# Routing of the second mixture shared out over four engines, and TensorE's joints filled with further rows and products

## The chip, the cores and the metric

The kernel runs on one core of one Trainium2 chip. The metric is the device time of one execution in microseconds (us). The core's engines are TensorE (PE; its weight loads are shown apart, as PEld), VectorE (DVE), ScalarE (ACT), GpSimd (POOL) and SyncE (SP), which issues DMAs. Each works through its own list of instructions in order and waits for others only through semaphores.

## The reference

An audio tower on 32 sequences of 166 positions (5312 tokens) of width 128, in float32:

```
h = tok(x)                          # three frames of 64, one dense layer
h = h + lru(norm(h))                # complex linear recurrence, 256 states
h = h + mixture0(norm(h))           # 16 experts, top 2
h = h + sparse_attention(norm(h))   # 8 heads, 25 chosen queries
h = h + mixture1(norm(h))           # 64 experts, top 42
```

`mixture0` picks two experts per token by `gate_logits`. For each expert it takes the mean of `silu(x w1)` over the expert's tokens, multiplies that mean by `w2`, and each token adds its two experts' results with its two routing weights. So its last step is a product of a 16 x 128 table `y_mean` and 16 weights per token.

`mixture1` is, for each token:

```
logits = x @ router_w + router_b                  # 64
probs = softmax(logits)
top_w, top_idx = top_k(probs, 42);  top_w = softmax(top_w)
comb = zeros(64).at[top_idx].set(top_w)
h = gelu(x @ w1[e] + b1[e]);  y = h @ w2[e] + b2[e]
out = sum over e of y[e] * comb[e]
```

## The kernel before, in words

Tokens lie along the free dimension: `k.h` and `k.hc` are 128 x 5376 (42 tiles of TW = 128 tokens; 14 chunks of CW = 384). `k.hc` holds the tokens less their mean, `k.rstd` one factor per token. The stages follow each other with all engines meeting between them. The order inside a stage is written out by hand: one function per engine, each a fixed list.

**The end of `first_mixture`.** ACT has put the tokens' 16 routing weights into rows 0 to 15 of `k.hc`, called `rt`. PE sums the table into bank 7 (L1105), DVE copies it to `ym`, 16 x 128 (L1048). Then PE multiplies `ym` by 384 tokens of `rt` for each of the 14 chunks (L1112), each into one of four banks, and DVE adds the bank to `k.h` (L1051). PE may be four chunks ahead. A float32 product appears as two instructions in the trace. After it comes `norm_statistics` "n3" (L411 to L449), in which POOL also splits experts' weights that SP fetches by DMA from the start of that stage (L1869 to L1877), and then the attention.

**The routing in `second_mixture`.** NP = 7 passes of two chunks (six tiles, PT) each. For a chunk c: POOL lays `rstd` on a diagonal (L778), PE spreads it over the partitions (L784), DVE multiplies it with `k.hc` to `ut` (`apply`, L792), ACT and POOL split `ut` into two float16 halves (`u_highs` L2109, `u_lows` L2073), and PE makes the 3 x 64 logits (`logits_of`, L2274). For a pass p, on DVE, in this order:

1. two copies of the logits out of the banks with the sign changed and the router's bias subtracted, into `row` (L2195), and the minimum of it (L2200);
2. `apply` of chunk 2p+2; the eight largest and their replacement (L2202, L2203); two small steps between ACT's two exponentials (L2205, L2206); `apply` of chunk 2p+3;
3. two more rounds of the eight largest and their replacement (L2209 to L2212), after which the 22 dropped experts carry a mark in `work`;
4. the masking of the exponentials by that mark (L2214), their sum (L2215) and its reciprocal (L2216). POOL multiplies them to `shares` (L2088).

ACT in pass p: first exponentials (L2125), `u_highs(2p+2)`, the copy of the turned shares of pass p-1 (L2113), the copy of the bias products of pass p-2 (L2117), second exponentials (L2135), `u_highs(2p+3)`.

PE's list in pass p: `logits_of(2p)`, spread of chunk 2p+2, `logits_of(2p+1)`, spread of chunk 2p+3, `turn(p-1)` (the transposes of the shares of pass p-1, L2283), `biases(p-2)` (the turned shares times `b2`, L2291). After pass 6 there follow `turn(6)`, `biases(5)` and `biases(6)`. `biases` of a pass waits until ACT has copied out those of the pass before.

**The expert loop** follows: 64 experts in four groups, six blocks of 896 tokens. PE multiplies up (`up_of`, L2322) and down (`down_of`, L2339), ACT, POOL and DVE do the gelu, the split into float16 halves and the sum. `WARM` is 8; `warm_up` is called at the start of some stages and multiplies constants into bank 7, which nobody reads.

Of the kernel before, what the change touches and what calls it, by code (L numbers as in the profile page):

```python
# [7 lines left out]
ALU = mybir.AluOpType  # L8
# [38 lines left out]
CUT = -2.5e38  # L47
# [24 lines left out]
def warm_up(nc, k):  # L72


    for _ in range(WARM):
        nc.tensor.matmul(k.bank[:, 7, :], k.sel[:, 0, :], k.sel[:, 0:4, :].rearrange("p a b -> p (a b)"), start=True, stop=True)
# [719 lines left out]
def first_mixture(nc, k):  # L796
# [6 lines left out]
    with ExitStack() as ctx:  # L803
# [40 lines left out]
        ym = sb("ym", [E0, 128])  # L844
        xt = sb("xt", [128, RING, 2, ST], F16)
        rt = k.hc[0:E0, :]

        gate_in = sem("gate_in")
        made = sem("made")
# [57 lines left out]
        @block.gpsimd  # L907
        def _(pool):
            g = nc.gpsimd
            g.memset(before[:], 1.0).then_inc(made, 1)  # L910
            g.memset(every[:], 1.0).then_inc(made, 1)
            g.memset(going[:], 1.0).then_inc(made, 1)
            g.memset(hsum[:], 0.0).then_inc(made, 1)
            g.iota(line[:], [[1, NST]], base=0, channel_multiplier=0, allow_small_or_imprecise_dtypes=True).then_inc(made, 1)
            g.iota(tile_no[:], [[0, 1]], base=0, channel_multiplier=1, allow_small_or_imprecise_dtypes=True).then_inc(made, 1)
            pool.wait_ge(made, 6)
            g.memset(going[:, :, 0:1], 0.0).then_inc(made, 1)
            g.affine_select(out=before[:], in_=before[:], compare_op=ALU.is_ge, fill=0.0, base=-1,
                            pattern=[[1, 128]], channel_multiplier=-1).then_inc(made, 1)
# [34 lines left out]
        def _(dve):  # L954
# [91 lines left out]
            v.tensor_copy(hsum[:, :, 0:E0 * E0:E0 + 1], k.bank[:, 1, 0:FC * E0].rearrange("p (f e) -> p f e", f=FC)).then_inc(gathered, 1)  # L1046
            dve.wait_ge(y_ready, 1)
            v.tensor_copy(ym[:], k.bank[0:E0, 7, 0:128]).then_inc(y_kept, 1)  # L1048
# [5 lines left out]
        def _(pe):  # L1054
# [54 lines left out]
            for c in range(NCW):  # L1109
                if c >= 4:  # L1110
                    pe.wait_ge(added, c - 3)
                t.matmul(k.bank[:, c % 4, 0:CW], ym[:], rt[:, span(c)], start=True, stop=True).then_inc(out, 1)  # L1112
# [835 lines left out]
def second_mixture(nc, k, out):  # L1948
# [9 lines left out]
    with ExitStack() as ctx:  # L1958
# [17 lines left out]
        rb = sb("rb", [128, E1])  # L1976
# [6 lines left out]
        ex = sb("ex", [128, 2, PT, E1])  # L1983
        shares = sb("shares", [128, NTW, E1])
# [18 lines left out]
        exp2 = sem("second_exp")  # L2003
        shared = sem("share_ready")
# [35 lines left out]
        @block.sync  # L2040
        def _(sp):
            for dst, src in ((router[:], a["router"]), (rb[:], a["router_b"].partition_broadcast(128)), (b1[:], a["e_b1"]),
                             (b2[:], a["e_b2"])):
                sp.dma_start(dst, src).then_inc(small_in, 16)

            def weights(grp):
                if grp >= 2:
                    sp.wait_ge(y_ready[1], (grp - 1) * NWB * GE + KEEP)
                for m in range(4):
                    sp.dma_start(k.weights[:, grp % 2, m], k.kept[grp - 1, :, m]).then_inc(group_in, 16)  # L2050

            def store(tb):

                cols = slice(tb * WB, min((tb + 1) * WB, T))
                sp.wait_ge(h_added, tb + 1)
                sp.dma_start(out[:, cols], k.h[:, cols]).then_inc(stored, 16)

            for grp in range(1, NG):
                weights(grp)
            for tb in range(NWB):  # L2060
                store(tb)
            sp.wait_ge(stored, 16 * NWB)

        @block.gpsimd
        def _(pool):
# [15 lines left out]

            ahead(0)
            ahead(1)
            for p in range(NP):
                ahead(2 * p + 2)
                ahead(2 * p + 3)
                pool.wait_ge(shared, p + 1)
                g.tensor_tensor(shares[:, p * PT:(p + 1) * PT], ex[:, p % 2], red[:, p % 2, 5].unsqueeze(2).broadcast_to([128, PT, E1]),  # L2088
                                ALU.mult).then_inc(share_ready, 1)
# [11 lines left out]
        def _(act):  # L2101
# [16 lines left out]

            u_highs(0)
            u_highs(1)  # L2120
            for p in range(NP):
# [15 lines left out]
                u_highs(2 * p + 3)  # L2137
            comb_copies(NP - 1)
# [23 lines left out]
        def _(dve):  # L2162
# [27 lines left out]
            for p in range(NP):  # L2190
                j = p % 2
                r = red[:, j]
                for q in range(2):
                    dve.wait_ge(logits, 2 * p + q + 1)
                    last = v.scalar_tensor_tensor(row[:, j, q * PT // 2:(q + 1) * PT // 2, 0:E1],  # L2195
                                                  k.bank[:, 4 + q, 0:PT // 2 * E1].rearrange("p (n e) -> p n e", e=E1), -1.0,
                                                  rb[:].unsqueeze(1).broadcast_to([128, PT // 2, E1]), ALU.mult, ALU.subtract)
                    last.then_inc(copied, 1)
# [3 lines left out]
                tiles(lambda m: v.max(best[:, m], row[:, j, m]))  # L2202
                tiles(lambda m: v.match_replace(work[:, m], best[:, m], row[:, j, m], MARK))  # L2203
# [3 lines left out]
                apply(2 * p + 3)  # L2207
                for last_round in (False, True):
                    tiles(lambda m: v.max(best[:, m], work[:, m]))  # L2209
                    if last_round:  # L2210
                        link(v.memset(best[:, :, drop % 8:8], SENT))
                    tiles(lambda m: v.match_replace(work[:, m], best[:, m], work[:, m], MARK))  # L2212
                dve.wait_ge(exp2, p + 1)
# [3 lines left out]
            dve.sem_inc(second_of[0], 2)  # L2217
            for q in range(2):
                dve.sem_inc(y_added[q], 1)
            dve.wait_ge(acc_ready, NP)  # L2220
# [9 lines left out]
            def add(it):  # L2230
# [3 lines left out]
                tb, e = it // GE % NWB, it // (GE * NWB) * GE + it % GE  # L2234
                for q, (start, end) in enumerate(PARTS_Y):
# [30 lines left out]
        def _(pe):  # L2266
            t = nc.tensor

            def logits_of(c):
# [3 lines left out]
                for q in range(CW // TW):  # L2273
                    last = t.matmul(k.bank[:, 4 + c % 2, q * E1:(q + 1) * E1], ut[:, c % 2, q * TW:(q + 1) * TW], router[:],  # L2274
                                    start=True, stop=True)
# [31 lines left out]
            turn(NP - 1)  # L2307
            biases(NP - 2)
            biases(NP - 1)
# [64 lines left out]

            pe.wait_ge(k.expert_weights.split, GROUP)
            pe.wait_ge(acc_ready, NP)
            pe.sem_inc(y_ready[1], KEEP)
            up_of(0, 0, 0, 0)
# [111 lines left out]
```

## Time and profile before

| | us |
|---|---|
| median of 3 runs | 2136.46 (2134.52 to 2138.97) |
| the profiled execution | 2138.86 |
| its span in the trace | 2137.1 |
| PE busy | 1885.2 (88%) |
| DVE busy | 1676.4 (78%) |
| ACT busy | 1388.1 (65%) |
| POOL busy | 1349.4 (63%) |

The span runs from the first to the last instruction of the trace; the time of the execution contains a little more around it. PEclk is the clock that was granted to TensorE as a share of full speed: 1.00 is 2.4 GHz and 0.50 is 1.2 GHz; a number between them is a mean over a stretch. In the timeline a row may stand for several like instructions (x6 and so on), the time is then from the first's start to the last's end, and brackets show how long the engine sat idle before it and who released it. "Issue" is idle time for which the trace shows no other engine.

### The profile page before, as it was taken

How to read it: one execution, taken by the hardware profiler on the slowest of the kernel's cores; microseconds unless marked ns; L12 is line 12 of the kernel's file. 1: busy time of each engine (PE TensorE's matmuls, PEld its weight loads, DVE VectorE, ACT ScalarE, POOL GpSimd, SP SyncE). 2: the span in 40 equal slices, each digit the busy share in tenths (PEclk: the TensorE clock that was granted, in tenths of full speed). 3: DMA queues.
4: the chain of work that ended last, by engine and by line, in shares of the span. 5: the costliest groups of instructions: out<-in, count | busy, mean ns of one | idle time of the engine just before them, and what ended most of it. 6: DMA issues, size and time to landing. Idle time of an engine off the chain costs nothing.

```text
span 2137.1 us, 50727 instructions
## 1 busy us (share of the span) xinstructions
PE 1885.2 (88%) x17146; PEld 1354.1 (63%) x17146; DVE 1676.4 (78%) x4764; ACT 1388.1 (65%) x2070; POOL 1349.4 (63%) x1026
## 2 busy tenths in 40 slices
PE   7889300888998987799999999999999999999998
PEld 5556200455657875567777777777777777777776
DVE  4775730853567767879999999999999999999998
ACT  3112350742443544488888888888888888888886
POOL 2100177005970003288989999988898989888887
PEclk9999655997998996599999999999999999999999
DMA  3612181612320002000000100000200000000000
GB/s 90 179 40 99 56 302 59 121 39 65 98 79 1 1 1 82 1 1 2 0 0 0 76 6 1 0 0 1 81 2 0 0 0 2 2 10 10 10 10 18
DMA packets 73497, 82.63 MB, mean 39 GB/s; under 512 B 38564, under 2 KB 56516, under 8 KB 71684
## 3 DMA queue, kind: packets, MB, share of 16 engines
q1 hardware_dynamic: 70660, 75.19, 11.6%
q0 software_dynamic: 2688, 5.44, 0.8%
q8 instruction: 94, 1.54, 0.3%
q14 instruction: 55, 0.45, 0.1%
HBM read 42.97 MB, written 29.20 MB: 34 GB/s over the span
## 4 chain that ended last, share of the span: by engine, by line
PE 56%; DVE 3%; issue 1%; POOL 0%; ACT 0%; ACTq 0%; DVEq 0%; POOLq 0%
PE bank L2339 29%; PE bank L2322 27%; DVE m_work L2212 1%; DVE m_best L2209 0%; DVE m_work L2203 0%; DVE m_ut L792 0%; PE bank L2291 0%; DVE m_best L2202 0%; DVE m_ex L2214 0%; ACT m_h L2153 0%; DVE h L2250 0%; POOL m_h L2098 0%; DVE m_red L2215 0%; DVE m_row L2195 0%; PE bank L784 0%
## 5 line engine op out<-in xcount | busy, mean ns | idle before, releaser
L2339 PEld LDWEIGHTS bank<-weights,m_h 128*128 128x128 f16 x10752 | 639.1, 98 | 190.0 <-DVE hc L2241 91.6
L2098 POOL TENSOR_TENSOR m_h<-m_hidden,m_h 128x896 f16<-128x896 f32 x384 | 725.2, 1888 | 31.9
L2241 DVE SCALAR_TENSOR_TENSOR hc<-bank,m_shares,hc 128x128 f32<-128x128 f32 x2688 | 727.0, 342 | 4.1 <-PE bank L2339 4.1
L2339 PE MATMUL bank<-weights,m_h 128*128 128x128 f16 x10752 | 724.4, 219 | 2.4 <-POOL m_h L2098 2.4
L2150 ACT ACTIVATE m_hidden<-bank,m_b 128x896 f32<-128x896 f32 x384 | 386.7, 1007 | 184.2 <-PE bank L2322 184.1
L2228 DVE TENSOR_TENSOR m_h<-bank,m_h 128x896 f16<-128x896 f32 x384 | 419.2, 1092 | 108.8 <-ACT m_h L2153 108.8
L2096 POOL TENSOR_SCALAR m_h<-m_hidden 128x896 f16<-128x896 f32 x384 | 359.8, 937 | 111.5 <-ACT m_hidden L2150 83.0
L2322 PE MATMUL bank<-m_u_first,weights 128*128 128x448 f16 (+1 forms) x1536 | 417.8, 354 | 6.9 <-DVE h L2250 5.5
L2322 PE MATMUL bank<-m_u_second,weights 128*128 128x448 f16 (+1 forms) x1536 | 417.4, 353 | 0.0
L2147 ACT ACTIVATE bank<-bank,m_b 128x896 f32<-128x896 f32 x384 | 377.2, 982 | 0.4 <-PE bank L2322 0.4
L2153 ACT ACTIVATE m_h<-bank 128x896 f16<-128x896 f32 x384 | 348.7, 908 | 0.0
L2322 PEld LDWEIGHTS bank<-m_u_second,weights 128*128 128x128 f16 x1536 | 150.5, 98 | 141.3 <-issue 1.8
L926 POOL DMA_INDIRECT expert_slots<-m_u_tok,m_slot x84 | 87.4, 1041 | 68.5 <-DVE m_slot L1018 43.2
L2322 PEld LDWEIGHTS bank<-m_u_first,weights 128*128 128x128 f16 x1536 | 118.1, 98 | 10.0 <-DVE h L2250 6.4
L1089 PE MATMUL bank<-m_xt,weights 128*128 128x384 f16 x344 | 65.6, 336 | 64.4 <-issue 64.4
L1042 DVE TENSOR_REDUCE m_part<-bank 128x2 f32<-128x768 f32 x86 | 74.7, 941 | 58.9 <-ACT bank L951 58.9
L2067 POOL MEMSET m_row<- 128x96 f32 x1 | 0.2, 178 | 185.7 <-POOLq L371 185.7
L951 ACT ACTIVATE bank<-bank 128x768 f32<-128x768 f32 x86 | 64.4, 794 | 64.4 <-PE bank L1089 64.4
L1089 PEld LDWEIGHTS bank<-m_xt,weights 128*128 x344 | 34.0, 99 | 96.2 <-issue 83.2
L1869 POOL CAST weights<-ew_raw 128x1024 f16<-128x1024 f32 x8 | 8.3, 1037 | 131.6 <-DMA ew_raw<-e_w_dram 131.6
L433 DVE TENSOR_TENSOR hc<-h,bank 128x332 f32 (+2 forms) x60 | 31.5, 525 | 52.8 <-PE bank L411 52.6
L543 POOL TENSOR_TENSOR lru_diag<-ident,rstd 128x332 f32<-128x332 f32 x16 | 12.8, 817 | 87.5 <-PE bank L684 61.6
(328 smaller groups left out, 2143.7 us busy)
## 6 DMA issues: line engine op xcount, KB each, us to landing
weights<-expert_factors SPq DMA_DIRECT2D x12, 1024.0 KB, 8.6
expert_slots<-lru_zeros SPq DMA_DIRECT2D x1, 8256.0 KB, 31.9
lw_raw<-e_w_dram SPq DMA_DIRECT2D x16, 512.0 KB, 4.8
expert_factors<-lw_made SPq DMA_DIRECT2D x16, 512.0 KB, 4.6
ew_raw<-e_w_dram SPq DMA_DIRECT2D x16, 512.0 KB, 4.4
lru_wst<-w_dram SPq DMA_DIRECT2D x16, 256.0 KB, 2.7
weights<-w_dram SPq DMA_DIRECT2D x1, 4096.0 KB, 12.7
expert_factors<-ew_made SPq DMA_DIRECT2D x8, 512.0 KB, 3.1
```

The source lines that it names most:

```text
L926: g.indirect_dma_start(out=k.slots, out_offset=bass.IndirectOffsetOnAxis(ap=slot[0:rows_n, m, n:n + 1], axis=0), in_=u_tok[0:rows_n, n].re ...
L1042: v.tensor_reduce(part[:, j // PARTS, j % PARTS * FP:(j % PARTS + 1) * FP], set_banks(j), X, ALU.add).then_inc(summed, 1)
L1089: last = t.matmul(set_banks(n)[:, f % FP], w0_parts[m][:, bass.ds(expert * FF0 + f * 128, 128)], xt[:, j % RING, m], start=(m == 0), stop= ...
L2096: g.tensor_scalar(h1[:, x, 0], hidden[:, x], 1.0 - SHARE, 1.0, ALU.mult, ALU.mult).then_inc(first_of[1], 1)
L2098: g.tensor_tensor(h1[:, x, 1], hidden[:, x], h1[:, x, 0], ALU.subtract).then_inc(second_of[1], 1)
L2147: sc.activation(banks0(x), banks0(x), ACT.Gelu, bias=b1[:, bass.ds(grp * GE + e, 1), 0]).then_inc(gelu[0], 1)
L2150: sc.activation(two(hidden[:, x % 2]), banks1, ACT.Gelu, bias=b1[:, bass.ds(grp * GE + e, 1), 1]).then_inc(gelu[1], 1)
L2153: sc.activation(two(h0[:, x, 0]), banks0(x), ACT.Copy, scale=1.0 - SHARE).then_inc(first_of[0], 1)
L2228: v.tensor_tensor(two(h0[:, x, 1]), banks0(it), two(h0[:, x, 0]), ALU.subtract).then_inc(second_of[0], 1)
L2241: last = v.scalar_tensor_tensor(acc[:, m * TW:(m + 1) * TW], y[q][:, (n - start) * TW:(n - start + 1) * TW], shares[:, m, e:e + 1], acc[:, ...
L2322: last = t.matmul(bank[:, q], k.weights[:, grp % 2, m, at], uu[:, bass.ds(tb * WB + q * HW, HW)], start=(m == 0), stop=(m == 1))
L2339: last = t.matmul(y[q][:, (n - start) * TW:(n - start + 1) * TW], factors[:, m, n * TW:(n + 1) * TW], k.weights[:, grp % 2, 2 + m, at], st ...
```

## The change

- `first_mixture`: `ym` becomes a 128 x 128 tile that POOL clears; the table is in its first 16 rows; the 14 products take all 128 rows of `k.hc` instead of `rt`.
- Routing: ACT copies the logits with the sign changed (`rows`), and PE adds the bias by a further product of one row per tile. For passes 0 to 5 POOL marks the kept experts and masks the exponentials; the sum and reciprocal of pass p-1 are done by DVE within pass p, behind its second `apply`, and POOL makes the shares of pass p-1 then. Pass 6 keeps the old order.
- The joint to the expert loop: PE's list is now `biases(5)`, 24 products of constants into bank 0, the first expert product, `turn(6)`, `biases(6)`. Semaphore increments and DVE's wait for the bias copies move.

Cut to its core:

```diff
-def warm_up(nc, k):
-    for _ in range(WARM):
-        nc.tensor.matmul(k.bank[:, 7, :], ...)
+def warm_up(nc, k, bank=7, count=WARM):
+    for _ in range(count):
+        nc.tensor.matmul(k.bank[:, bank, :], ...)
# first_mixture
-        ym = sb("ym", [E0, 128])
+        ym = sb("ym", [128, 128])
+            g.memset(ym[:], 0.0).then_inc(cleared, 1)
+            dve.wait_ge(cleared, 1)
-            v.tensor_copy(ym[:], k.bank[0:E0, 7, 0:128]).then_inc(y_kept, 1)
+            v.tensor_copy(ym[0:E0], k.bank[0:E0, 7, 0:128]).then_inc(y_kept, 1)
-                t.matmul(k.bank[:, c % 4, 0:CW], ym[:], rt[:, span(c)], start=True, stop=True).then_inc(out, 1)
+                t.matmul(k.bank[:, c % 4, 0:CW], ym[:], k.hc[:, span(c)], start=True, stop=True).then_inc(out, 1)
# second_mixture, SP: (rb[:], a["router_b"].partition_broadcast(128)) becomes (rb[:], a["router_b"]), rb [1, E1]
# POOL
+            def shares_of(p):
+                pool.wait_ge(shared, p + 1)
+                g.tensor_tensor(shares[...], ex[:, p % 2], red[:, p % 2, 5]..., ALU.mult).then_inc(share_ready, 1)
             for p in range(NP):
                 ahead(2 * p + 2)
+                if p:
+                    shares_of(p - 1)
                 ahead(2 * p + 3)
-                pool.wait_ge(shared, p + 1)
-                g.tensor_tensor(shares[...], ...).then_inc(share_ready, 1)
+                if p < NP - 1:
+                    pool.wait_ge(chosen, p + 1)
+                    pool.wait_ge(exp2, p + 1)
+                    g.tensor_scalar(kept[:], work[:, :, 0:E1], CUT, 1.0, ALU.is_gt, ALU.mult).then_inc(marked, 1)
+                    pool.wait_ge(marked, p + 1)
+                    g.tensor_tensor(ex[:, p % 2], kept[:], ex[:, p % 2], ALU.mult).then_inc(masked, 1)
+            shares_of(NP - 1)
# ACT
+            def rows(p):
+                for q in range(2):
+                    act.wait_ge(logits, 2 * p + q + 1)
+                    sc.activation(row[...], k.bank[:, 4 + q, ...], ACT.Copy, scale=-1.0).then_inc(copied, 1)
+            rows(0)
             for p in range(NP):
                 ...
                 u_highs(2 * p + 3)
+                rows(p + 1)
# DVE
             for p in range(NP):
-                for q in range(2):
-                    dve.wait_ge(logits, 2 * p + q + 1)
-                    last = v.scalar_tensor_tensor(row[...], k.bank[:, 4 + q, ...], -1.0, rb[:]..., ALU.mult, ALU.subtract)
-                    last.then_inc(copied, 1)
                 dve.wait_ge(copied, 2 * p + 2)
                 ...
+                if p:
+                    dve.wait_ge(marked, p)
                 tiles(lambda m: v.match_replace(work[:, m], best[:, m], row[:, j, m], MARK))
                 ...
                 apply(2 * p + 3)
+                if p:
+                    dve.wait_ge(masked, p)
+                    link(v.tensor_reduce(red[:, 1 - j, 4], ex[:, 1 - j], X, ALU.add))
+                    v.reciprocal(red[:, 1 - j, 5], red[:, 1 - j, 4]).then_inc(shared, 1)
                 for last_round in (False, True):
                     ...
+                if p < NP - 1:
+                    dve.sem_inc(chosen, 1)
+                    continue
                 dve.wait_ge(exp2, p + 1)
                 ...
-            dve.sem_inc(second_of[0], 2)
-            dve.wait_ge(acc_ready, NP)          # now in add(), before its first sum
# PE
-                    last = t.matmul(k.bank[...], ut[...], router[:], start=True, stop=True)
+                    t.matmul(tile, ut[...], router[:], start=True, stop=False)
+                    last = t.matmul(tile, k.ones[0:1, :], rb[:], start=False, stop=True)
-            turn(NP - 1)
-            biases(NP - 2)
-            biases(NP - 1)
+            biases(NP - 2)
             pe.wait_ge(k.expert_weights.split, GROUP)
+            pe.wait_ge(u_low, NCW)
+            pe.sem_inc(second_of[0], 2)
+            pe.sem_inc(y_ready[1], KEEP)
+            warm_up(nc, k, 0, 3 * WARM)
+            up_of(0, 0, 0, 0)
+            turn(NP - 1)
+            biases(NP - 1)
             pe.wait_ge(acc_ready, NP)
-            pe.sem_inc(y_ready[1], KEEP)
-            up_of(0, 0, 0, 0)
```

## Rows read from the trace of the kernel before

**Rows 1.** the page, parts 2 (tenths of full clock in 40 slices) and 4 (the chain)

```profile
PEclk9999655997998996599999999999999999999999
...
PE bank L2339 29%; PE bank L2322 27%; DVE m_work L2212 1%; DVE m_best L2209 0%; DVE m_work L2203 0%; DVE m_ut L792 0%; PE bank L2291 0%; DVE m_best L2202 0%; DVE m_ex L2214 0%; ACT m_h L2153 0%; DVE h L2250 0%; POOL m_h L2098 0%; DVE m_red L2215 0%; DVE m_row L2195 0%; PE bank L784 0%
```

**Rows 2.** windows, first joint (length, busy of PE, PEld, DVE, ACT, POOL, PEclk)

```profile
476.00:478.00 2.00, 1.83 (x6) 1.14 (x7) 0.91 (x3) 0.00 (x0) 0.00 (x0) 1.00 0.00 0
480.00:493.00 13.00, 12.37 (x20) 5.90 (x18) 5.70 (x11) 0.00 (x0) 0.00 (x0) 0.50 0.00 0
```

**Rows 3.** windows of one routing pass and of the first expert products

```profile
867.18:878.73 11.55, 10.02 (x35) 7.33 (x34) 11.14 (x66) 6.41 (x22) 4.22 (x5) 0.50 0.00 1
909.70:915.10 5.40, 5.37 (x15) 2.14 (x16) 0.17 (x1) 4.50 (x6) 0.79 (x1) 0.50 0.00 0
```

**Rows 4.** timeline of the same routing pass (start, us, engine, line, instruction)

```profile
867.18 0.58 DVE L2195 SCALAR_TENSOR_TENSOR m_row<-bank,m_rb 128x192 f32<-128x192 f32 x2
...
867.80 0.55 DVE L2200 TENSOR_REDUCE m_red<-m_row 128x6 f32<-128x384 f32 x1
...
868.23 1.49 PE L2283 MATMUL bank<-ident,m_shares 128*64 128x128 f32 x6 [0.49 <-POOL m_shares L2088]
...
868.38 0.35 ACT L2125 ACTIVATE m_ex<-m_row,m_red 128x64 f32<-128x64 f32 x1 [4.12 <-DVE m_red L2200]
...
870.39 0.51 ACT L2109 ACTIVATE m_u_first<-m_ut 128x384 f16<-128x384 f32 x1
...
871.82 0.54 DVE L792 TENSOR_TENSOR m_ut<-hc,bank 128x384 f32<-128x384 f32 x1
...
872.50 1.54 PE L2274 MATMUL bank<-m_router,m_ut 128*128 128x64 f32 x6
...
873.84 1.59 PE L784 MATMUL bank<-m_diag,ones 128*128 128x384 f32 x2
...
875.22 1.38 PE L2274 MATMUL bank<-m_router,m_ut 128*128 128x64 f32 x6
...
876.98 1.02 DVE L2214 SCALAR_TENSOR_TENSOR m_ex<-m_work,m_ex 128x384 f32<-128x384 f32 x1
...
878.04 0.55 DVE L2215 TENSOR_REDUCE m_red<-m_ex 128x6 f32<-128x384 f32 x1
...
878.89 0.83 POOL L2088 TENSOR_TENSOR m_shares<-m_ex,m_red 128x384 f32<-128x384 f32 x1 [1.31 <-DVE m_red L2216]
```

**Rows 5.** timeline, minima of passes 1 and 6, and the last joint

```profile
833.61 0.55 DVE L2200 TENSOR_REDUCE m_red<-m_row 128x6 f32<-128x384 f32 x1
...
890.43 0.55 DVE L2200 TENSOR_REDUCE m_red<-m_row 128x6 f32<-128x384 f32 x1
...
893.52 0.90 DVE L2209 MAX8 m_best<-m_work 128x8 f32<-128x72 f32 x6
...
905.88 2.90 PE L2291 MATMUL bank<-m_b,m_comb 64*128 64x128 f32 x12 [0.99 <-ACT hc L2117]
...
909.73 0.90 PE L2322 MATMUL bank<-m_u_first,weights 128*128 128x448 f16 x2 [0.95 <-issue]
...
911.17 0.95 PE L2322 MATMUL bank<-m_u_first,weights 128*128 128x448 f16 x2
```

**Rows 6.** timeline around the first joint

```profile
477.12 1.84 DVE L1051 TENSOR_TENSOR h<-h,bank 128x384 f32<-128x384 f32 x3 [1.00 <-PE bank L1112]
...
492.40 0.56 DVE L1051 TENSOR_TENSOR h<-h,bank 128x384 f32<-128x384 f32 x1 [0.72 <-PE bank L1112]
...
515.30 2.12 POOL L1877 TENSOR_TENSOR weights<-ew_left,weights 128x1024 f16<-128x1024 f32 x1
...
518.01 0.22 DVE L449 TENSOR_TENSOR rstd<-n_st 83x64 f32<-83x64 f32 x1
```

**Rows 7.** weight loads of L1112 and L2274 (duration ns min/median/max)

```profile
L1112 PEld LDWEIGHTS bank<-hc,m_ym x28: 181/328/328, 476.2 to 490.9; 16*128 16x128 f32 x28
...
L2274 PEld LDWEIGHTS bank<-m_router,m_ut x84: 186/333/338, 818.7 to 886.4; 128*128 128x128 f32 x84
```

More of the change, by code:

```diff
@@ L69, in load_table @@
     nc.scalar.activation(k.cells[:, n + 1:n + 2], k.cells[:, 0:1], function)
-def warm_up(nc, k):
-    for _ in range(WARM):
-        nc.tensor.matmul(k.bank[:, 7, :], k.sel[:, 0, :], k.sel[:, 0:4, :].rearrange("p a b -> p (a b)"), start=True, stop=True)
+def warm_up(nc, k, bank=7, count=WARM):
+    for _ in range(count):
+        nc.tensor.matmul(k.bank[:, bank, :], k.sel[:, 0, :], k.sel[:, 0:4, :].rearrange("p a b -> p (a b)"), start=True, stop=True)
 STEP = 4
@@ L848, in first_mixture @@
         gate_in = sem("gate_in")
+        cleared = sem("outputs_cleared")
         made = sem("made")
@@ L1975, in second_mixture @@
         router = sb("router", [128, E1])
-        rb = sb("rb", [128, E1])
+        rb = sb("rb", [1, E1])
         b1 = sb("b1", [128, E1, HC])
@@ L1983, in second_mixture @@
         ex = sb("ex", [128, 2, PT, E1])
+        kept = sb("kept", [128, PT, E1])
         shares = sb("shares", [128, NTW, E1])
@@ L2003, in second_mixture @@
         exp2 = sem("second_exp")
+        marked = sem("kept_marked")
+        masked = sem("dropped_masked")
+        chosen = sem("dropped_marked")
         shared = sem("share_ready")
@@ L2041, in _ @@
         def _(sp):
-            for dst, src in ((router[:], a["router"]), (rb[:], a["router_b"].partition_broadcast(128)), (b1[:], a["e_b1"]),
+            for dst, src in ((router[:], a["router"]), (rb[:], a["router_b"]), (b1[:], a["e_b1"]),
                              (b2[:], a["e_b2"])):
@@ L2080, in ahead @@
                     norm.pool_diagonal(pool, c + 2, c % 2)
+            def shares_of(p):
+                pool.wait_ge(shared, p + 1)
+                g.tensor_tensor(shares[:, p * PT:(p + 1) * PT], ex[:, p % 2], red[:, p % 2, 5].unsqueeze(2).broadcast_to([128, PT, E1]),
+                                ALU.mult).then_inc(share_ready, 1)
             ahead(0)
@@ L2085, in _ @@
                 ahead(2 * p + 2)
+                if p:
+                    shares_of(p - 1)
                 ahead(2 * p + 3)
-                pool.wait_ge(shared, p + 1)
-                g.tensor_tensor(shares[:, p * PT:(p + 1) * PT], ex[:, p % 2], red[:, p % 2, 5].unsqueeze(2).broadcast_to([128, PT, E1]),
-                                ALU.mult).then_inc(share_ready, 1)
+                if p < NP - 1:
[5 more added lines that the diff above has]
+            shares_of(NP - 1)
             with pool.Fori(0, NG * NWB * GE // 2) as i:
@@ L2117, in biases @@
                 sc.activation(two(acc[:, 2 * p * CW:2 * (p + 1) * CW]), k.bank[:, 6:8, 0:CW], ACT.Copy).then_inc(acc_ready, 1)
+            def rows(p):
+                if p >= NP:
+                    return
+                for q in range(2):
+                    act.wait_ge(logits, 2 * p + q + 1)
+                    sc.activation(row[:, p % 2, q * PT // 2:(q + 1) * PT // 2, 0:E1],
+                                  k.bank[:, 4 + q, 0:PT // 2 * E1].rearrange("p (n e) -> p n e", e=E1), ACT.Copy,
+                                  scale=-1.0).then_inc(copied, 1)
             u_highs(0)
             u_highs(1)
+            rows(0)
             for p in range(NP):
@@ L2192, in _ @@
                 r = red[:, j]
-                for q in range(2):
-                    dve.wait_ge(logits, 2 * p + q + 1)
-                    last = v.scalar_tensor_tensor(row[:, j, q * PT // 2:(q + 1) * PT // 2, 0:E1],
-                                                  k.bank[:, 4 + q, 0:PT // 2 * E1].rearrange("p (n e) -> p n e", e=E1), -1.0,
-                                                  rb[:].unsqueeze(1).broadcast_to([128, PT // 2, E1]), ALU.mult, ALU.subtract)
-                    last.then_inc(copied, 1)
                 dve.wait_ge(copied, 2 * p + 2)
@@ L2234, in add @@
                 tb, e = it // GE % NWB, it // (GE * NWB) * GE + it % GE
+                if it == 0:
+                    dve.wait_ge(acc_ready, NP)
                 for q, (start, end) in enumerate(PARTS_Y):
@@ L2273, in logits_of @@
                 for q in range(CW // TW):
-                    last = t.matmul(k.bank[:, 4 + c % 2, q * E1:(q + 1) * E1], ut[:, c % 2, q * TW:(q + 1) * TW], router[:],
-                                    start=True, stop=True)
+                    tile = k.bank[:, 4 + c % 2, q * E1:(q + 1) * E1]
+                    t.matmul(tile, ut[:, c % 2, q * TW:(q + 1) * TW], router[:], start=True, stop=False)
+                    last = t.matmul(tile, k.ones[0:1, :], rb[:], start=False, stop=True)
                 last.then_inc(logits, 1)
```

## The prediction

> **What bounds the kernel now.** The page comes first: the chain that ended last lies for 29% and 27% of the span on the two TensorE lines of the expert loop, every other line has 1% or less [rows 1]. That loop runs from about 921 us to the end at the full clock (the trailing 9s of the PEclk row) with PE busy without a gap, and the change touches no instruction of it. What can move is in the places where the PEclk row shows 5s. I read two of them in windows and then in the timeline.
>
> The first is the joint at the end of the first mixture. PE enters it at granted clock 1.00, and while it multiplies operands of only 16 rows it is busy in 12.37 of 13.00 us at 0.50 [rows 2]: the clock fell under an engine that hardly ever waited. There VectorE waits for PE once per chunk.
>
> The second is the routing before the expert loop, seven passes p. In a window of one pass in the middle VectorE is busy 11.14 of 11.55 us; PE is busy 10.02 of them, at 0.50 [rows 3]. The timeline of the same pass gives the prices [rows 4]. So VectorE is the bound, but PE at its slow rate has only 1.5 us of slack, and this decides the forecast. After the last pass PE, ACT and POOL hand on to each other until the first expert product at 909.73 [rows 5].
>
> **The change, part by part.**
>
> *First joint.* The 14 products get 128 rows instead of 16 (the further rows meet zero weights). Three adds at the full rate take 1.84 us, so (1.84 - 0.56) / 2 = 0.64 us per chunk; the last add now ends at 492.40 + 0.56 = 492.96 [rows 6]. If PE stays at full clock, the last ends at 477.12 + 13 x 0.64 + 0.56 = 486.00: 7.0 us earlier. The next stage, the third normalisation, then also starts at full clock, but POOL's weight pieces in it hang on a DMA issued after the joint: they end at 517.42 and VectorE's last step at 518.23 [rows 6], so POOL is late next and only 0.8 us more can be kept. Together -7.8. Bounds: 0 (zero weights count for nothing and the clock falls as before) and -7.8. I take -7.8: up to 478 the clock is still 1.00, carried by products of 128 rows, and only the rows differ. The clearing of the larger tile on POOL is awaited some 250 us later: nothing.
>
> *Routing, VectorE's own work.* Each pass loses two bias-adding copies (867.18 to 867.80: 0.62) and, in the first six, the masking (876.98 to 878.04: 1.06, where the work of a single 384-element instruction, 0.55 as in the reduce behind it, fills half) [rows 4]. So 9.87 instead of 11.55 if VectorE stayed the bound. POOL takes over with a marking and a masking of 384 elements, 0.4 (bound 0.83) + 0.83; it is idle then and has them ready long before VectorE asks.
>
> *Routing, the cycle that closes.* Before, the share of pass p-1 was ready at the end of pass p-1, so PE could turn it and multiply the biases while VectorE began pass p. Now its sum comes in the middle of pass p, after the second `apply`. PE's order is unchanged: the turn of p-1 and the biases of p-2 stand ahead of the logits of chunks 2p+2 and 2p+3, and pass p+1 cannot start without those. So one pass becomes a loop through all engines, each term from [rows 4]:
> - the last logit to VectorE through ACT's copy of 192 elements: 0.46 with hand-offs (an exponential of 64 takes 0.35, a copy of 384 takes 0.51; nearer the middle);
> - VectorE from the minimum (867.80) to the end of the second `apply` (871.82 + 0.54 = 872.36): 4.56;
> - sum and reciprocal until POOL starts, 878.04 to 878.89: 0.85; POOL's share 0.83 and its hand-off to PE 0.06: 0.89;
> - turn and biases, 868.23 to 872.50: 4.27;
> - logits: six instructions take 1.34 (872.50 to 873.84). Each product gets a partner of one row, so twelve: 2.68;
> - spread of rstd, 873.84 to 875.22: 1.38; the second logits 2.72.
>
> Sum 17.81 us instead of 11.55. The price of the one-row products is not shown. From below it is 0; from above the 0.24 of a bias product (12 in 2.90 [rows 5]). A weight load of 16 rows takes 328 ns and one of 128 rows 333 [rows 7]: rows don't make it cheaper, so I take the 0.223 of a router product.
>
> From p=1 to p=2 there are no biases yet (14.95), three passes are full, from p=5 to p=6 no spread is left (16.43): 14.95 + 3 x 17.81 + 16.43 = 84.8, against 890.43 - 833.61 = 56.8 now [rows 5]. That is +28.0, and +14.6 with free one-row products. The first pass has no earlier share to wait for; its later logits (about +1.1) and its lighter work cancel: 0.
>
> *Last joint.* Now: from the last minimum 890.43 to PE's first expert product 909.73, 19.3 us [rows 5]. After: VectorE reaches the rounds 3.09 later (893.52), sum and share 1.74, so PE's turn starts at 4.83; turn and biases 9.1; ACT copies them out before PE may go on, 1.0 (the idle time in the row of 905.88); the biases of p=5 until 13.0. Then 24 warm-up products of 512 columns. Four expert products of 448 columns start within 911.17 - 909.73 = 1.44 us at 0.50 [rows 5], 0.36 each, so one of 512 takes 0.41; that dense stretch stayed at 0.50 for 5.4 us [rows 3]. So 13 warm-up products are slow and 11 take half: 7.7, until 20.7. The first expert products 0.8, the turn 0.7 (until 22.2), ACT's two copies with hand-offs 1.8, the last biases 1.4 at full clock (2.9 at half), ACT's copy 0.9: 26.3 instead of 19.3, so +7.0. The warm-up stands ahead of the last turn in PE's queue, and the share it needs is ready about 6 us before PE gets there. A warm start gives back about 1.0 of the 5.4 us ramp (bounds 0 and 2.7, if all of it were PE's own).
>
> The moved waits and semaphore increments and the smaller bias load (the pass starts on a later DMA anyway) cost nothing.
>
> Sum: -7.8 + 28.0 + 7.0 - 1.0 = +26.2. The profiled execution took 2138.86 us (span 2137.1 and 1.8 around it), 2.4 above the median of the runs; 2136.46 + 26.2 = 2163.
>
> **A rule of the skill against this.** In [rows 4] PE works without a break from the turn at 868.23 to the end of the second logits near 876.6, and the window has 0.50 throughout [rows 3]. The Trainium skill, page "TensorE: Matmul & The Clock Gate", section "Why this matters for your kernels", says that steady work releases the clock and that only long gaps between bursts bring it down. By that rule PE's unbroken run in the new pass, 11 us, would go at full rate; the trace doesn't bear it out, with longer busy shares than the new loop has.
>
> **The rivals.**
> - *PE at full clock in the routing.* For it: the stretch is longer and unbroken. Against it: PE's share falls to 12.4 of 17.8 us (70%, now 87% at 0.50), and half of the added products have one row, while 16 rows lost the clock in [rows 2]. PE's terms halve (11.05 to 5.5): 12.3 per full pass, 59.4 for the five, so +2.6; last joint 19.9, +0.6; -1.0; -7.8: -5.6, 2131. If the clock is full for only part of each pass, half-way: 2147.
> - *VectorE stays the bound* (the late share finds PE free). It needs the turn not to stand ahead of logits that the next pass waits for; the order in the code says it does. About 1.5 less per pass, -7.5; +7.0; -1.0; -7.8: -9.3, 2127.
> - *The rows don't hold the clock*: the joint's 7.8 stay away, 2171. For it: most of the weights are zero.
> - *One-row products cost nothing*: 2163 - 13.4 = 2150.
>
> The sign turns where the loop is shorter than about 12.5 us.
>
> **How the numbers follow.** The low-clock loop has 0.83, with the joint failing in 0.12 of it and cheap one-row products in 0.05; partly full clock 0.07; full clock 0.05; VectorE the bound 0.05. Range 2148 to 2171: from cheap products (or a partly full clock) to the failing joint. A measurement tells about 0.2% (4.3 us) from no change. Faster: the last two cases, with little from the third, 0.09; within 0.2%: 0.03; slower: 0.88.
>
> **What would show it.** In the changed profile: L1112 with a chunk every 0.64 us and granted clock 1.00; in the routing PEclk 0.5 and a minimum of row every 17 to 18 us, VectorE waiting for ACT's copies there and ACT for PE's logits; PE's turn of the last share starting 6.3 us behind the minimum instead of beside it; a warm-up of 24 at the end with the last turn behind it. It is wrong if the passes are 12.5 us or less apart, or if PEclk in the routing is near 1.

## The result, and the profile after

| | before | after |
|---|---|---|
| median of 4 runs each, us | 2135.94 (2134.52 to 2138.97) | 2176.72 (2173.63 to 2193.05) |
| the profiled execution | 2138.86 | 2173.63 |
| its span | 2137.1 | 2171.9 |
| PE / DVE / ACT / POOL busy | 1885.2 / 1676.4 / 1388.1 / 1349.4 | 1911.7 / 1667.7 / 1394.0 / 1365.2 |

The ratio is 1.0178, with a 95% interval from 1.0138 to 1.0218: slower, as forecast, but by 40.8 us where 26.2 were forecast, and outside the range. The two profiled executions lie 34.8 apart. Without a head start that the change did not make it would be 40.2: the copy of the table `ym` starts at 470.47 after and at 475.84 before, 5.4 earlier, though ahead of it only POOL's clearing of the tile was added (in the profiles of the other kernels it starts anywhere between 470.7 and 493.0).

The page of the changed kernel, parts 2 and 4, answers to [rows 1]:

```profile
PEclk9999655998989985589999999999999999999999
...
PE bank L2372 28%; PE bank L2355 26%; PE bank L2311 1%; PE bank L2310 1%; PE bank L2327 1%; PE bank L784 1%; PE bank L2319 0%; DVE m_work L2230 0%; PE bank L76 0%; DVE m_best L2227 0%; POOL m_shares L2093 0%; DVE m_ut L792 0%; ACT m_h L2184 0%; DVE h L2285 0%; POOL m_h L2118 0%
```

Before, the first lines behind the expert loop were VectorE's; now they are PE's one-row product (L2311), router product (L2310), bias product (L2327) and spread (L784). Part 1 says the same: VectorE lost 8.7 us of work and PE gained 26.5.

The windows of the changed kernel (columns as in [rows 2] and [rows 3]): the first joint, the first routing pass up to its minimum, one pass in the middle, and the start of the expert loop in steps of 5 us:

```profile
471.70:480.70 9.00, 8.40 (x27) 4.61 (x25) 7.76 (x14) 0.00 (x0) 0.00 (x0) 1.00 0.00 0
804.60:813.70 9.10, 9.10 (x28) 7.00 (x27) 0.56 (x1) 1.29 (x4) 3.35 (x4) 0.50 1.00 419
860.24:879.88 19.64, 14.60 (x47) 10.69 (x47) 9.49 (x63) 7.18 (x24) 6.71 (x7) 0.50 0.00 0
935.00:940.00 5.00, 5.00 (x25) 2.48 (x23) 0.00 (x0) 0.00 (x0) 0.00 (x0) 0.90 0.00 0
940.00:945.00 5.00, 2.42 (x15) 1.84 (x14) 0.00 (x0) 2.62 (x4) 0.00 (x0) 0.79 0.00 0
945.00:950.00 5.00, 4.62 (x13) 1.40 (x12) 1.09 (x1) 4.78 (x7) 1.65 (x2) 0.53 0.00 0
```

A pass takes 19.64 us instead of 11.55, with no engine busy for more than 14.60 of them: a loop through all engines, and not one engine's work. The timeline of that loop, PE first, then ACT, VectorE and POOL:

```profile
846.82 1.49 PE L2319 MATMUL bank<-ident,m_shares 128*64 128x128 f32 x6 [5.04 <-POOL m_shares L2093]
848.23 2.93 PE L2327 MATMUL bank<-m_b,m_comb 64*128 64x128 f32 x12
851.09 0.69 PE L2310 MATMUL bank<-m_router,m_ut 128*128 128x64 f32 x2
851.71 0.69 PE L2311 MATMUL bank<-m_rb,ones 1*128 1x64 f32 x2
852.32 0.69 PE L2310 MATMUL bank<-m_router,m_ut 128*128 128x64 f32 x2
...
854.79 1.65 PE L784 MATMUL bank<-m_diag,ones 128*128 128x384 f32 x2
856.23 0.53 PE L2310 MATMUL bank<-m_router,m_ut 128*128 128x64 f32 x2
...
859.77 1.65 PE L784 MATMUL bank<-m_diag,ones 128*128 128x384 f32 x2
...
859.87 0.33 ACT L2144 ACTIVATE m_row<-bank 128x192 f32<-128x192 f32 x1 [4.65 <-PE bank L2311]
...
860.24 0.55 DVE L2225 TENSOR_REDUCE m_red<-m_row 128x6 f32<-128x384 f32 x1 [9.84 <-ACT m_row L2144]
...
864.26 0.54 DVE L792 TENSOR_TENSOR m_ut<-hc,bank 128x384 f32<-128x384 f32 x1
864.73 0.54 DVE L2238 TENSOR_REDUCE m_red<-m_ex 128x6 f32<-128x384 f32 x1
...
865.57 0.83 POOL L2093 TENSOR_TENSOR m_shares<-m_ex,m_red 128x384 f32<-128x384 f32 x1 [0.46 <-DVE m_red L2239]
```

The brackets close the loop: PE waits 5.04 us for POOL's share, ACT 4.65 for PE's last logits, VectorE 9.84 for ACT's copy, and POOL waits for VectorE's sum. Where the 40.2 us lie, by the starts of the same instruction in both traces:

| stretch | before | after | difference | forecast |
|---|---|---|---|---|
| `ym` copy to rstd of the second mixture | 475.84 to 814.44 | 470.47 to 800.40 | -8.7 | -7.8 |
| rstd to the first minimum | 8.09 | 13.33 | +5.2 | 0 |
| passes 0 to 1 | 11.08 | 10.38 | -0.7 | 0 |
| passes 1 to 6 | 56.82 | 93.77 | +37.0 | +28.0 |
| last minimum to the expert loop | 19.30 | 26.85 | +7.6 | +7.0 |
| the expert loop to the end | 1227.4 | 1227.2 | -0.2 | -1.0 |

### The profile page after: what moved, and what is told of

Same layout as the page of the kernel before. It is cut to its first block, busy times and chain, and to the rows that moved or that the text cites. A ratio compares the mean times of both kernels' runs of the same rounds, so it can differ in the third digit from the quotient of the medians.

```text
span 2171.9 us, 50963 instructions
## 1 busy us (share of the span) xinstructions
PE 1911.7 (88%) x17254; PEld 1374.7 (63%) x17254; DVE 1667.7 (77%) x4744; ACT 1394.0 (64%) x2084; POOL 1365.2 (63%) x1039
## 4 chain that ended last, share of the span: by engine, by line
PE 59%; DVE 1%; issue 1%; ACT 1%; POOL 1%; ACTq 0%; DVEq 0%; POOLq 0%
PE bank L2372 28%; PE bank L2355 26%; PE bank L2311 1%; PE bank L2310 1%; PE bank L2327 1%; PE bank L784 1%; PE bank L2319 0%; DVE m_work L2230 0%; PE bank L76 0%; DVE m_best L2227 0%; POOL m_shares L2093 0%; DVE m_ut L792 0%; ACT m_h L2184 0%; DVE h L2285 0%; POOL m_h L2118 0%
```

## The experiments

Baselines: the kernel before took 2137.95 beside full_row_bias, paired_bias, bias_dve and lag, 2137.54 beside joint1, joint1_tail, lag_bias_dve_tail and no_warm, and 2137.07 beside old_share and joint1_64. The diffs are cut to their core. A product means one call in the code, which is two instructions in the trace. Two theories stand at the start. *Change of rows*: a product of one row costs more than its like when it stands between products of 128. *Accumulation*: a second product into the same bank region costs more, whatever its rows. A third, *the clock*, would blame the granted clock, but that is 0.50 in the pass of before and of after alike.

**full_row_bias**: the changed kernel, with the router's bias in row 0 of a zeroed tile of 128 rows.

```diff
-        rb = sb("rb", [1, E1])
+        rb = sb("rb", [128, E1])            # cleared, the bias in row 0
-                    last = t.matmul(tile, k.ones[0:1, :], rb[:], start=False, stop=True)
+                    last = t.matmul(tile, k.ones[:], rb[:], start=False, stop=True)
```

> The changed kernel, but the bias product has 128 rows: ones of 128 rows against a tile with the bias in row 0 and zeros below. In the changed kernel three router products with their one-row partners take 3.68 us where twelve instructions of equal price would take 2.68. Theory 'change of rows' (each change between 128-row and 1-row weights costs some 0.17 us): 2.68 per chunk, minima of the middle passes 17.6 us apart instead of 19.64, the execution some 10 us shorter. Theory 'accumulation' (the second product waits for the first in the same tile): nothing moves, 3.68 and 19.64.

Measured: 2162.99 in one run. The middle passes are 17.55 us apart (17.56, 17.55, 17.55). PE's rows of this kernel, to be held beside those of the changed one above:

```profile
851.36 0.63 PE L2314 MATMUL bank<-m_rb,ones 128*128 128x64 f32 x2
851.78 0.63 PE L2313 MATMUL bank<-m_router,m_ut 128*128 128x64 f32 x2
852.21 0.64 PE L2314 MATMUL bank<-m_rb,ones 128*128 128x64 f32 x2
```

Like product follows like after 0.42 us, where it was 0.62 with one row. With 127 rows of zeros more, the kernel is some 14 us faster. A chunk's six products (three of the router, three of the bias) take 2.61 (850.88 to 853.49) instead of 3.70 (851.09 to 854.79). The accumulation is as before, so that theory is out. The weight loads show the same. First the changed kernel, then this one:

```profile
851.70 0.50 PEld L2311 LDWEIGHTS bank<-m_rb,ones 1*128 1x128 f32 x2
852.32 0.50 PEld L2310 LDWEIGHTS bank<-m_router,m_ut 128*128 128x128 f32 x2
```

```profile
851.25 0.55 PEld L2314 LDWEIGHTS bank<-m_rb,ones 128*128 128x128 f32 x2
851.68 0.55 PEld L2313 LDWEIGHTS bank<-m_router,m_ut 128*128 128x128 f32 x2
```

Where the rows change, the load starts together with its own product (851.70 and 851.71), when the product before is all but over (851.09 + 0.69 = 851.78, an end that the profile models). Where all have 128, it starts 0.11 ahead of its product (851.25 and 851.36) and lies beside the one before. That the late load is what costs the time is not shown; the two go together.

**paired_bias**: one-row products, but the middle tile in the opposite order (router, bias, bias, router, router, bias), which leaves four changes of rows per chunk instead of six.

```diff
+                    first, then = (ut[...], router[:]), (k.ones[0:1, :], rb[:])
+                    if q == 1:
+                        first, then = then, first
+                    t.matmul(tile, *first, start=True, stop=False)
+                    last = t.matmul(tile, *then, start=False, stop=True)
```

> The changed kernel with the order of the two products turned round in the middle tile of each chunk (router, bias, bias, router, router, bias): four changes of rows per chunk instead of six, the same accumulations. 'Change of rows': 0.34 us less per chunk, minima 18.95 apart, some 3.5 us shorter. 'Accumulation': 19.64, no shorter.

Measured: 2174.98 in one run, 1.7 below the changed kernel's median where 3.5 were expected, too little to read from one run; the middle passes are 18.88 apart (18.95 expected). Three kernels give three points: 0, 4 and 6 changes per chunk, 2.61, 3.32 and 3.70 us per chunk. That is 0.18 us for each change, twice: 0.71 / 4 and 1.09 / 6. The theory of the changes of rows holds with its number, for one row among products of 128; no other pair of row counts was tried.

**bias_dve**: the changed kernel with the logits copied and biased by VectorE, as before the change; the late share, POOL's mask and both joints stay.

```diff
-            rows(0)
-                rows(p + 1)
-                    last = t.matmul(tile, k.ones[0:1, :], rb[:], start=False, stop=True)
+                for q in range(2):
+                    dve.wait_ge(logits, 2 * p + q + 1)
+                    last = v.scalar_tensor_tensor(row[...], k.bank[:, 4 + q, ...], -1.0, rb[:]..., ALU.mult, ALU.subtract)
```

> The changed kernel with the bias back on VectorE: its two copies per pass as before, no one-row products, no copies on ACT; masking on POOL and the late share stay. Theory 'the loop through the late share sets the pass': router products 1.34 per chunk, minima 19.64 - 2 x 2.34 + 0.1 = 15.1 us apart, the five passes 23 us shorter and the first some 4 us, so about 2149. Rival 'the one-row products are all of the loss, the late share is harmless': VectorE is the bound again at 10.5 to 10.9 per pass, about 2128.

Measured: 2150.9 in two runs, ratio 1.0074 (1.0045 to 1.0103); passes of 15.61, 15.02, 15.02. The late share closes the loop alone; the change of sign does not need the one-row products.

**old_share**, the complement: the kernel before with only ACT's copies and the one-row products.

```diff
+            def rows(p):                     # ACT, as in the changed kernel
-                for q in range(2):           # the two copies on DVE
-                    last = t.matmul(k.bank[...], ut[...], router[:], start=True, stop=True)
+                    t.matmul(tile, ut[...], router[:], start=True, stop=False)
+                    last = t.matmul(tile, k.ones[0:1, :], rb[:], start=False, stop=True)
```

> The kernel before with one part of the change alone: ACT copies the logits, PE adds the bias by one-row products; the share stays at the end of its pass, masking on VectorE, both joints as before. The one-row products' measured price adds 2.36 us per chunk to TensorE (3.70 for the logits of a chunk instead of 1.34), so its 10.02 us per pass become 14.7. By 'TensorE's own work is then the bound' the minima stand 14.7 to 15.2 us apart in the middle passes, and the time is about 2155. By 'the bias products lie in slack that only the late share takes away' the minima stay near 11.6 and the time near 2140. By the forecast's price (1.34 per chunk) they would stand about 12.7 apart, 2144.

Measured: 2147.36, ratio 1.0047 (1.0025 to 1.0068); passes 1 to 6 are 11.31, 11.81, 14.39, 14.40 and 13.11 apart. The profiled execution was a long one (2159.74; its routing starts some 11 us later than before's), so only the passes are read from it. Its windows and a few rows:

```profile
850.00:865.00 15.00, 15.00 (x56) 11.10 (x56) 13.77 (x88) 9.20 (x32) 5.34 (x7) 0.61 0.00 1
865.00:880.00 15.00, 15.00 (x49) 11.16 (x48) 13.31 (x81) 7.58 (x26) 6.19 (x7) 0.50 0.00 1
880.00:900.00 20.00, 20.00 (x64) 14.85 (x64) 12.38 (x72) 8.62 (x32) 5.40 (x7) 0.50 0.01 2
```

```profile
863.08 0.43 PE L2281 MATMUL bank<-m_rb,ones 1*128 1x64 f32 x2
863.44 0.43 PE L2280 MATMUL bank<-m_router,m_ut 128*128 128x64 f32 x2
...
867.08 0.69 PE L2281 MATMUL bank<-m_rb,ones 1*128 1x64 f32 x2
867.70 0.69 PE L2280 MATMUL bank<-m_router,m_ut 128*128 128x64 f32 x2
```

PE is the bound here, busy without a gap, and 14.40 is its own work (10.02 [rows 3] and twice 3.70 - 1.34 give 14.7). The passes before are shorter for two reasons: 11.31 (at 0.50) has no biases yet, and 11.81 has the PE instructions of a full pass, with part of them at the high clock (0.64 over that pass; 0.36 from one product to the next instead of 0.62). So the time came out at 2147 and not near 2155. The four kernels make a square of middle passes: neither part 11.55, one-row products alone 14.40, late share alone 15.02, both 19.64. Alone, the one-row products cost 2.85, since 1.5 us of them go into time that PE had free. With the loop closed they stand on the path, all twelve instructions: 19.64 - 15.02 = 4.62, 0.385 each.

**lag**: the changed kernel, with turns, biases and their copies one pass later in PE's and ACT's lists, so that PE finds each share ready. ACT's first exponentials also wait for the shares of pass p-2, whose place they take.

```diff
-                if p:
-                    turn(p - 1)
-                if p >= 2:
-                    biases(p - 2)
+                if p >= 2:
+                    turn(p - 2)
+                if p >= 3:
+                    biases(p - 3)
```

> The changed kernel with the turns, the biases and ACT's copies of them moved one pass later in the lists (in pass p the turn of p-2 and the biases of p-3), so that no logits stand behind a share that is still being made. PE has the same products. Theory 'loop': the pass falls from 19.64 to PE's own work, 1.41 + 2.86 + 2 x 3.68 + 2 x 1.4 = 14.5 us; 22 us shorter over the passes, perhaps 2 to 4 given back in the tail, so about 2157. Rival 'PE's added work sets the pass by itself': minima stay about 19 apart, 2175.

Measured: 2142.34, ratio 1.0016 (0.9998 to 1.0035); passes 1 to 6 are 10.38, 10.01, 11.35, 14.39 and 13.11 apart. (The profiled execution took 2159.81; its copy of `ym` starts only at 493.0, so again only the routing is read from it.) The steady pass is PE's own work, as expected; the total came out 15 us better. One part is the clock: the pass of 11.35, at 0.65, has the PE instructions of the one of 14.39, at 0.50. Another is that the early passes are lighter in this order: 10.38, at 0.50, has no turn and no biases. Windows of this kernel:

```profile
850.00:860.00 10.00, 9.91 (x32) 7.13 (x31) 9.15 (x61) 5.31 (x22) 6.60 (x7) 0.51 0.01 2
860.00:870.00 10.00, 9.58 (x37) 6.96 (x37) 9.55 (x64) 6.25 (x24) 6.72 (x7) 0.66 0.00 1
870.00:880.00 10.00, 10.00 (x41) 7.32 (x40) 8.24 (x52) 5.61 (x17) 6.72 (x7) 0.67 0.00 1
880.00:890.00 10.00, 10.00 (x36) 7.77 (x34) 8.00 (x57) 5.83 (x19) 5.36 (x6) 0.50 0.01 2
```

All but 4.4 of the 40.8 us are gone by the order of two lists (and the higher clock that part of it was granted), with every instruction of the change still there: the loop, and not the work, was most of the price.

**joint1**: the kernel before with the first joint's 128 rows alone (diff as in the change).

> The kernel before with the first joint alone changed: the cleared 128-row tile and all 128 rows of hc. Theory 'rows hold the clock': the 14 chunks take 0.64 us each at granted clock 1.00 and the execution is 8 us shorter (7.0 in the joint, 1 in the stage behind it), ratio 0.9963. Rival 'the gain is given back in the next stage, where POOL waits for its DMA': under 3 us.

Measured: 2130.66, ratio 0.9961 (0.9937 to 0.9984). This part is a gain of 6.9 us. **joint1_64** takes 64 rows:

```diff
-                t.matmul(k.bank[:, c % 4, 0:CW], ym[:], k.hc[:, span(c)], ...)
+                t.matmul(k.bank[:, c % 4, 0:CW], ym[0:64], k.hc[0:64, span(c)], ...)
```

> The kernel before with the first joint's products of 64 rows (48 of them with zero weights) instead of 16 or 128. If any number of rows above 16 holds the clock, the granted clock stays 1.00 and the 14 chunks take 8.9 us. If half the rows count for half, the clock falls on the way, and the joint takes between 10 and 15.8 us (15.8 is what 16 rows took).

Measured: 2131.84 in one run. The joint in the timeline and two windows of this kernel:

```profile
477.00 8.94 DVE L1054 TENSOR_TENSOR h<-h,bank 128x384 f32<-128x384 f32 x14 [1.00 <-PE bank L1115]
```

```profile
480.00:484.00 4.00, 4.00 (x14) 2.34 (x13) 3.46 (x7) 0.00 (x0) 0.00 (x0) 1.00 0.00 0
484.00:488.00 4.00, 2.65 (x10) 1.41 (x9) 1.99 (x5) 1.49 (x2) 0.00 (x0) 1.00 0.21 26
```

64 rows, 48 of them with zero weights, hold the clock as 128 do; 16 do not [rows 2].

**no_warm**: the changed kernel without the 24 warm-up products (the call of `warm_up(nc, k, 0, 3 * WARM)` deleted).

> The changed kernel without the 24 warm-up products. Theory 'the warm-up stands in front of the last turn': the turn of pass 6 starts when its share is ready, at half clock; from the last minimum to the first expert product behind the copies 21.5 us instead of 26.85, 5.3 us shorter than the changed kernel, about 2170. Rival 'the warm-up pays for itself at full clock': not shorter, 2175 or more.

Measured: 2167.56 in two runs, ratio 1.0129 (1.0081 to 1.0178), 9.2 less than the changed kernel, with an interval about as wide; the traces tell more: from the last minimum (917.61) to the expert loop (937.55) 19.94 us instead of 26.85, and from there to the end 1226.3 instead of 1227.2. The warm-up costs its 6.9 us and gives nothing back.

**joint1_tail**: joint1, with the last joint in the new order but without warm-up, and with ACT's gelu table loaded ahead of the last shares.

```diff
# ACT
-            comb_copies(NP - 1)
             biases(NP - 2)
+            load_table(nc, k, 0, ACT.Gelu)
+            comb_copies(NP - 1)
             biases(NP - 1)
             act.sem_inc(second_of[1], 2)
-            load_table(nc, k, 0, ACT.Gelu)
# PE: biases(5), up_of(0, 0, 0, 0), turn(6), biases(6)
```

> The kernel before with the first joint, and with the last joint in another order and without warm-up products: the biases of pass 5 as soon as PE is free, then the first expert product, then the turn and the biases of pass 6; ACT loads the gelu table before it waits for the last turn. The routing passes are as before. Theory 'the chain behind the last share is what costs, and nothing may stand in front of it': from the last minimum to the first gelu 16.4 us instead of 21.1, so 4.7 shorter than the first joint alone, about 2125. Rival 'the order hardly matters, ACT's copies are late anyway': under 1.5.

Measured: 2123.8, ratio 0.9922 (0.9893 to 0.9951). The last joint of this kernel:

```profile
889.31 2.89 PE L2294 MATMUL bank<-m_b,m_comb 64*128 64x128 f32 x12 [0.99 <-ACT hc L2120]
892.13 0.93 PE L2322 MATMUL bank<-m_u_first,weights 128*128 128x448 f16 x2
...
893.66 1.14 PE L2286 MATMUL bank<-ident,m_shares 128*64 128x128 f32 x6
895.69 1.60 PE L2294 MATMUL bank<-m_b,m_comb 64*128 64x128 f32 x12 [0.89 <-ACT m_comb L2116]
898.19 0.93 PE L2322 MATMUL bank<-m_u_first,weights 128*128 128x448 f16 x2 [0.90 <-ACT hc L2120]
```

```profile
893.07 1.28 ACT L69 ACT_TABLE_LOAD   x1
...
897.33 0.81 ACT L2120 ACTIVATE hc<-bank 128x768 f32<-128x768 f32 x1 [1.69 <-PE bank L2294]
898.03 0.98 ACT L2150 ACTIVATE bank<-bank,m_b 128x896 f32<-128x896 f32 x1
```

From the last minimum (883.54) to the first gelu 14.5 us; 21.1 before (890.43 to 911.52), 28.2 after (917.88 to 946.09). The 1.28 us table load now lies in ACT's idle time, and the biases of the last pass run at a granted clock of 1.00 (1.60 us instead of 2.90). The clock doesn't stay: the expert products behind them start 0.36 us apart again, as at 0.50.

**lag_bias_dve_tail**: joint1_tail's joints, the late share, POOL's mask, the lag, and the bias on VectorE (the diffs of bias_dve, lag and joint1_tail together).

> All that the runs point to: the first joint, masking on POOL with the late share, turns and biases one pass later in the lists, the bias on VectorE, no one-row products, no warm-up, and the gelu table loaded before the last turn. Theory 'loop': VectorE is the bound again, at 11.55 - 1.06 = 10.5 us per pass, PE's 10.0 beside it; the five passes take about 53 us instead of 56.8. The tail has turn 5 and biases 4 and 5 in front of turn 6 and gains nothing on before. About 2125. Rival: PE at 10 of 10.5 us becomes the bound through its waits and the passes stay at 11 or more, 2130.

Measured: 2123.66, ratio 0.9924 (0.9895 to 0.9953); passes of 10.66 instead of 11.55, but 19.0 us from the last minimum to the first gelu, since a lagging pass is left over. Both last kernels beat the kernel before and after and can't be told from each other.

## Why the prediction was wrong in size

**What held.** The sign, the bound (a loop through PE, VectorE, POOL and ACT at half clock) and most of its terms. Measured in the changed kernel against the forecast: last logit to minimum 0.47 (0.46), minimum to the end of the second `apply` 4.56 (4.56), sum until POOL starts 0.84 (0.85), turn and biases 4.27 (4.27), spread 1.44 (1.38). The kernel in which a one-row product costs what the forecast took for it, full_row_bias, took 2162.99 with passes of 17.55: forecast 2163 and 17.81. That the totals agree so closely is luck: it is one run, and in it the first pass cost 1.6 us more than the forecast's 0 and the five passes 1.5 less (83.34 instead of 84.8). The first joint went at 1.00 in 8.94 us (8.88 forecast). With free one-row products 15.13 per pass were forecast, and bias_dve shows 15.02.

**The step that failed** is the price of the one-row products: "rows don't make it cheaper, so I take the 0.223 of a router product". It asked only whether few rows make a product cheaper, from the duration of its weight load [rows 7], and took 0 and 0.24 as its ends. These are prices of one instruction. Measured, the six one-row instructions of a chunk add 3.70 - 1.34 = 2.36 us, 0.39 each, above the upper end. A duration of one instruction was taken for its price in a row of others; all rows of before that gave a price stood among their like, and no row bounded a product between unlike ones. It adds (19.64 - 17.81) = 1.8 per full pass and 9.0 over passes 1 to 6. The first pass adds 4.5, the last joint 0.6 and the ramp 0.8, and the first stretch takes 0.9 off: 14.0, which is 40.2 less 26.2.

**The first pass** is a second term that failed: it was put at 0, its later logits against lighter work; it came to +5.2 and -0.7. Its twelve one-row instructions stand on the path at 0.50, before there is anything else to hide behind: joint1, with no partner and 0.50 there too, needs 5.10 from its first logits (810.28) to its first minimum (815.38), the changed kernel 9.10 (804.63 to 813.73), so +4.0. The other 1.25 is the clock: the kernel before needs only 3.85 (818.68 to 822.53). The windows of that stretch, first of before, then of joint1, which has the same instructions there:

```profile
818.68:822.53 3.85, 3.17 (x16) 2.62 (x16) 1.27 (x4) 0.58 (x2) 3.35 (x4) 0.87 0.95 389
```

```profile
810.28:815.38 5.10, 4.79 (x16) 3.81 (x16) 1.27 (x3) 0.54 (x2) 3.36 (x4) 0.50 0.96 397
```

In the profiles of the eleven other kernels of this case the same stretch comes at other times; ten show 0.50 and one 0.76 (old_share). So the kernel before had a high clock here that was lost when the work moved. But the same kernels differ the other way one stage earlier, at the start of the second mixture's normalisation (before, then the changed kernel):

```profile
792.68 4.35 PE L411 MATMUL bank<-h,mean_w 128*128 128x384 f32 x8 [0.84 <-DVEq L429]
```

```profile
780.18 2.82 PE L411 MATMUL bank<-h,mean_w 128*128 128x384 f32 x8 [0.84 <-DVEq L429]
```

Before had 0.65 in those 4.35 us, the changed kernel 1.00. The two kernels with the higher clock in the first pass, before and old_share, are the two that take 4.35 and 4.37 here; the ten others take 2.82. So 1.5 us were won in one stage and 1.25 lost in the next, by a clock that rose at another time. Why it does was not settled.

**The last joint** cost 7.6 (7.0): the warm-up took 7.90 (7.7). **The ramp** gave 0.2 instead of 1.0. The forecast let the clock that the warm-up had raised live through the hand-offs behind it. In the windows above it stands at 0.90, then 0.79 while PE is busy for 2.42 of 5.00 us, then 0.53 when the loop starts. no_warm shows it from the other side: without the warm-up the loop starts 6.9 us earlier and the kernel is 9.2 us shorter.

**The first stretch** gave 0.9 more than forecast. The joint and the normalisation behind it gave 7.4 (475.84 to 518.01 before, 470.47 to 505.28 after; 7.8 forecast), and the normalisation of the second mixture 1.5, by its clock as shown above. joint1's medians say 6.9 in all, with the 1.25 taken off.

**The marking on POOL** took 1.50 us and the mask 0.99 (forecast 0.4, at most 0.83, and 0.83). POOL had the time, as argued, so it cost nothing.

**The rivals.** None came. The nearest, *full clock in the routing*, fell by the 0.50 of the window; lag and old_share show that it was no idle one, with 0.61 to 0.67 over 10 to 15 us where PE works without a gap. The Trainium skill ("TensorE: Matmul & The Clock Gate", "Why this matters for your kernels") would have steady work keep the full rate. By the rows of old_share that is not enough here: 20.00 of 20.00 us busy at 0.50.

In medians, each against the kernel before beside it: the first joint alone -6.9; the change without one-row products (bias_dve, the joint's gain included) +13.0; the whole change +40.8. So the one-row products cost 27.8, where the forecast had 13.4 for them.

## What to carry to other kernels

- Price an added product in the row it will stand in, not by its like elsewhere: where its number of rows differs from its neighbours', pad it with zero rows, or put equals next to each other. This case shows it for one row among 128.
- Before a wait is moved within a pass, write the loop that it closes through the in-order lists; a list that takes the work one pass later can open it at no cost in instructions.
- A warm-up can be lost when hand-offs follow it (here it stood at 0.53 when the loop began), and a gain in one stage can shift the next into another clock: read PEclk of the stages behind it too.

## What the runs showed of the hardware

- A float32 product of one row between products of 128 rows, at 1.2 GHz: 0.18 us for each change of rows (2.61, 3.32 and 3.70 us per six products with 0, 4 and 6 changes). Its weight load takes no longer (median 308 ns, 333 with 128 rows), but starts with its product and not 0.11 us ahead. The Trainium skill, page "TensorE: Matmul & The Clock Gate", section "LDWEIGHTS (loading the stationary operand)", says that a load goes by its columns and not by its rows; these medians agree to within 8%.
- The granted clock fell to 0.50 with 16-row operands at 12.37 of 13.00 us busy [rows 2], and stayed at 1.00 with 64 and with 128 rows, most with zero weights, at 4.00 of 4.00 and 8.40 of 9.00.
- With a mix of short products (1, 64 and 128 rows, and transposes), PE busy without a gap was granted 0.61 in one stretch of 15 us and 0.50 in the next 35 (old_share).
- Eight instructions of 384 columns at the start of one stage took 4.35 us at 0.65 in one kernel and 2.82 at 1.00 in another, though nothing in that stage or in the one ahead of it was changed.
- POOL's comparison of 384 elements took 1.50 us, its product of 384 elements 0.83 to 0.99.
